# Scores ahead of values, masks and exponentials ahead of the split of the output, in every unit of an attention group

## What is computed

```python
q = (x @ w_q) ...            # 32 heads of 128; k, v: 8 heads, shared by 4 query heads
lk = (x @ w_lq @ w_lk) ...   # 32 latent keys; lv = (x @ w_lv), 32 latent values
q, k, lk = rope(q), rope(k), rope(lk)
attn = causal_softmax(q, k, v)       # s = q k^T * scale, masked, softmax, times v
lat = causal_softmax(q, lk, lv)
x = layernorm(x + attn @ w_o + lat @ w_lo)
```

## Time and profile before

| | |
|---|---|
| median of the runs | 2509.61 us |
| the profiled execution | 2513.95 us, of which the span of instructions is 2512.0 us |
| PE busy | 2453.2 us, 98% of the span |
| PE weight loads | 2067.0 us, 82% |
| DVE busy | 1717.3 us, 68% |
| ACT busy | 1132.0 us, 45% |
| POOL busy | 923.3 us, 37% |
| granted TensorE clock, mean | 0.995 of full speed |
| DMA | 226.24 MB, mean 90 GB/s |

### The profile page before, as it was taken

How to read it: one execution, slowest core, us unless ns; L and a number is a source line. 1 busy time by engine, 2 the same in 40 slices (tenths; PEclk the granted TensorE clock), 3 DMA queues, 4 the chain that set the end, 5 groups by cost and what they waited for, 6 DMA issues and landing times.

```text
span 2512.0 us, 40346 instructions
## 1 busy us (share of the span) xinstructions
PE 2453.2 (98%) x12264; PEld 2067.0 (82%) x12264; DVE 1717.3 (68%) x3589; ACT 1132.0 (45%) x2576; POOL 923.3 (37%) x696
## 2 busy tenths in 40 slices
PE   7799999999999999999999999999999999999998
PEld 6688888888888888888767888888888888888877
DVE  5676667767676767666577676766767677667656
ACT  3443535344444435444365453544445353544550
POOL 4334242433334242433443425243342425334210
PEclk9999999999999999999999999999999999999999
DMA  5223231322323232323424323222232323234411
GB/s 172 93 80 97 60 106 53 98 64 70 94 76 96 61 101 61 87 68 99 129 86 133 105 70 110 69 86 77 84 104 71 106 73 106 61 93 144 155 34 67
DMA packets 124406, 226.24 MB, mean 90 GB/s; under 512 B 13088, under 2 KB 21408, under 8 KB 124192
## 3 DMA queue, kind: packets, MB, share of 16 engines
q1 hardware_dynamic: 119552, 216.91, 28.8%
q10 hardware_dynamic: 4768, 8.39, 1.0%
HBM read 206.37 MB, written 18.87 MB: 90 GB/s over the span
## 4 chain that ended last, share of the span: by engine, by line
PE 93%; DVE 2%; issue 1%; ACT 1%; DMA 1%; POOL 1%; SPq 0%; PEldq 0%; DVEq 0%; ACTq 0%; POOLq 0%
PE bank_a L1217 16%; PE bank_a L1218 16%; PE bank_a L1219 16%; PE bank_b L1217 13%; PE bank_b L1219 13%; PE bank_b L1218 13%; PE bank_b L1270 5%; DMA w_raw<-wstream 1%; PE bank_b L1539 1%; POOL w_lo L426 1%; DVE probs L821 0%; POOL acc L445 0%; PE bank_b L1406 0%; ACT w_hi L490 0%; PE bank_b L1522 0%
## 5 line engine op out<-in xcount | busy, mean ns | idle before, releaser
L426 POOL TENSOR_TENSOR w_lo<-w_raw,w_hi 128x512 fp32r<-128x512 f32 x632 | 845.0, 1346 | 1400.1 <-ACT w_hi L490 1380.4
L490 ACT ACTIVATE w_hi<-w_raw 128x512 fp32r<-128x512 f32 x632 | 392.7, 626 | 298.0 <-DMA w_raw<-wstream 115.3
L1217 PE MATMUL bank_a<-w_hi,o_hi 128*128 128x512 f32 x1024 | 410.2, 401 | 4.1 <-DVE o_lo L843 2.0
L1218 PE MATMUL bank_a<-w_lo,o_hi 128*128 128x512 f32 x1024 | 401.8, 392 | 0.0
L1219 PE MATMUL bank_a<-w_hi,o_lo 128*128 128x512 f32 x1024 | 401.6, 392 | 0.0
L527 ACT ACTIVATE probs<-probs,row_min 128x512 f32<-128x512 f32 (+3 forms) x512 | 281.6, 552 | 245.6 <-DVE row_min L821 243.1
L838 DVE TENSOR_TENSOR pT_lo<-bank_b,pT_hi 128x512 fp32r<-128x512 f32 (+1 forms) x384 | 207.2, 595 | 238.0 <-ACT pT_hi L533 238.0
L537 ACT ACTIVATE o_hi<-bank_b 128x512 fp32r<-128x512 f32 x128 | 76.8, 600 | 452.0 <-PE bank_b L1219 452.0
L832 DVE TENSOR_SCALAR probs<-probs,row_inv 128x512 f32<-128x512 f32 (+3 forms) x512 | 260.9, 569 | 4.5
L1217 PE MATMUL bank_a<-xT_hi,w_hi 128*128 128x512 f32 x544 | 215.7, 396 | 18.0 <-POOL w_lo L426 15.2
L1219 PEld LDWEIGHTS bank_a<-w_hi,o_lo 128*128 128x128 f32 x1024 | 192.6, 188 | 41.5
(11 more groups left out here) (168 smaller groups left out, 4686.5 us busy)
## 6 DMA issues: line engine op xcount, KB each, us to landing
w_raw<-wstream SPq DMA_DIRECT2D x632, 256.0 KB, 2.7
stage<-ctx SPq DMA_DIRECT2D x32, 256.0 KB, 2.8
stage_w<-wf SPq DMA_DIRECT2D x32, 256.0 KB, 2.8
q_scratch<-stage_q SPq DMA_DIRECT2D x32, 128.0 KB, 1.7
wf_hi_scratch<-piece_hi SPq DMA_DIRECT2D x16, 256.0 KB, 3.0
wf_lo_scratch<-stage_w SPq DMA_DIRECT2D x16, 256.0 KB, 3.4
wf_hi<-wf_hi_scratch SPq DMA_DIRECT2D x8, 512.0 KB, 7.6
wf_lo<-wf_lo_scratch SPq DMA_DIRECT2D x8, 512.0 KB, 8.1
```

Source lines behind the costliest of these rows:

```text
L426: nc.gpsimd.tensor_tensor(w_lo[:, s], w_raw[:, r], w_hi[:, s].bitcast(F32), ALU.subtract).then_inc(lo_done, 1)
L490: nc.scalar.activation(w_hi[:, s], w_raw[:, r], ACT.Copy).then_inc(hi_done, 1)
L1217: nc.tensor.matmul(dst, still[0], move[0], start=start, stop=False)
L1218: nc.tensor.matmul(dst, still[0], move[1], start=False, stop=False)
```

## The change

Three pairs of calls change places, each in every unit. On PE the scores of unit u + 2 go ahead of the values of unit u, with the transposes and both parts where they were. On DVE the masks of unit u + 2 go ahead of the low part of the output of unit u. On ACT the exponentials of unit u + 2 go ahead of the high part of the output of unit u. Unit 6 has values and no scores to make, unit 7 neither, and both stay as they were. No instruction is added or removed, and no wait is written differently.

```diff
--- before.py
+++ after.py
@@ -677,8 +677,8 @@
                         if c % 2 == 0:
                             pT_high(G, u)
                         else:
+                            exponentials(G, u + 2) if u + 2 < UNITS else None
                             o_high(G, u)
-                            exponentials(G, u + 2) if u + 2 < UNITS else None
                         if b and not tg:
                             crossed(c)
                     if b and c in (12, 29):
@@ -989,10 +989,10 @@
                         add_part(b, p + u // 2, u // 2, chunk(b, g, C_PREV + 4 + 2 * u), False)
                     if u in (4, 6):
                         add_part(b, p + u // 2, u // 2 - 2, chunk(b, g, C_PREV + 4 + 2 * u), first)
+                    if u + 2 < UNITS:
+                        mask_scores(G, u + 2)
                     if u + 1 < UNITS:
                         o_low(G, u)
-                    if u + 2 < UNITS:
-                        mask_scores(G, u + 2)
                     if u < 2 and first and b:
                         for t in range(TT):
                             half_stats_of_r(t, u)
@@ -1464,9 +1464,10 @@
                     transposes(G, u)
                     if u < UNITS - 1:
                         part(2 * u + 3)
-                        values(G, u)
                     if u + 2 < UNITS:
                         scores(G, u + 2)
+                    if u < UNITS - 1:
+                        values(G, u)
 
             def last_output(b, i):
```

## The result

The changed kernel took 2500.36 us (median of five runs, 2496.32 to 2501.99). Five runs of the kernel before beside it gave 2510.13 (2509.36 to 2513.61). The ratio is 0.9955, with an interval of 0.9941 to 0.997: 7.5 to 14.8 us faster, around 11.3. Forecast were 7.5 us and 2502.1, with 2500.4 as the low end of the range. (The forecast counted from 2509.61, the median of three of these five runs.)

The account below looks back on a forecast made before the run. PE, busy 98% of the span, was taken as the bound, with gain from its waits in the two first groups. 5.4 + 0.9 + 1.2 = 7.5 us off the median 2509.61 gave 2502.1, range 2500.4 to 2506.5.

Parts of the forecast that it names:

- 5.4 for batch 0: Batch 0's first group: S(6) starts 5.4 us before the time V(4) had, a lead carried to the end.
- Batch 1's term of 0.9: Batch 1's first group: 0.9 us gained by S(6), which was V(4); bounds -0.6 and 2.2.
- S(4) starts 0.6 later than V(2) did: Batch 1's first group: o_low waits for ACT's exponentials, so pT_low(2) ends at 1324.1, not 1323.5, and S(4) starts 0.6 later.
- The mask wait is hidden, and o_low takes its place in part: First groups: V(u) covers the masks' 1.78 us; new waits of 0.3 to 1.8 us on o_low before O(1), O(2), O(3).
- 1.55 more: O(0) in batch 0's first group: 2.87 us at full clock instead of 4.41, besides starting 1.55 earlier.
- the clock falls all the same: Rival, chance 0.25: O(0) in batch 0 still runs at half speed; the gain there is 3.9 instead of 5.4, total 2503.6.
- I take the clock as kept: Batch 0's first group: one gap of 1.7 remains, dense matmuls until 107.5, so O(0) runs at full clock.
- The 14 other groups, 1.2: Ordinary groups: V(1)'s weights get pT_low(1) net 0.09 us sooner, 14 times, so 1.2 us; bounds 0 and 1.8.
- about 0.2 instead of 0.29: Sign: in other groups S(3)'s weights wait about 0.2 us for pT_low(1), where V(1)'s had waited 0.29.
- group period unchanged to 0.1: Sign that the forecast is right: the period of the groups stays unchanged to 0.1 us.
- the 0.05 behind the values: PE: the block after V pays 0.05; now the part instead of S, so nothing; if both paid, 112 units, 5.6 worse.
- Slower: Rival, chance 0.08: in the 14 groups o_high delays pT_high(1), V(1)'s place moves 0.52 later in each; 2515.4 at worst.

Follow-up runs that it names:

- after: The profiled execution of the changed kernel, with all three exchanges in every unit: 2501.99 us.
- after_again: The changed kernel run once more, unedited, on another chip: 2499.53 us, ratio 0.9954 to the kernel before.
- rest_only: The kernel before with the three exchanges in the 14 ordinary groups alone, the old order in the two first groups: 2507.17 us, ratio 0.9986.
- before_pool_late: The kernel before, with POOL's low part of chunk 32 in batch 1's first group held until DVE has clipped the weight piece: 2508.0 us (one run).
- pe_dve: The kernel before with the exchanges on PE and DVE, ACT keeping o_high ahead of the exponentials: 2507.28 us (one run).
- dve_act_only: The kernel before with the exchanges on DVE and ACT, PE keeping values ahead of scores: 2521.79 us (one run).
- before: The profiled execution of the kernel before, with the old order everywhere: 2513.95 us.
- before_warm: The kernel before with 8 extra matmuls into an unused bank ahead of T(0) in both first groups: 2509.32 us, ratio 0.9995.

## Why the prediction came out as it did

**Which step failed.** The waits went and came as forecast; two terms of the sum were too small. The range's low end was added up from 5.4 for batch 0, 2.2 for batch 1 and 1.8 for the 14 other groups, the last two at their bounds. The stretches of the 14 groups gave 2.95, beyond their bound: the prediction counted one place per ordinary group, and neither the same place in unit 5 of the first groups nor any other step. Batch 1's term of 0.9, with its step "S(4) starts 0.6 later than V(2) did", measured 1.96: S(4) came 0.45 sooner. The 0.04 us by which the median lies below the range are themselves far inside the noise.

**The mask wait is hidden, and o_low takes its place in part: right.** In batch 0 T(1) to T(4) lost their waits of 1.06 to 1.42 (the first two in the earlier trace rows), and O(1) to O(3) wait 0.61, 0.30 and 0.61 in batch 0 and 0.62, 0.34 and 1.19 in batch 1, inside the forecast 0.3 to 1.8. The steps to O(1) in after, first DVE, then ACT:
```profile
113.86 0.69 DVE L821 CUSTOM_DVE_ANT_0 probs<-bank_b,mask_sb 128x512 f32<-128x512 f32 x1 [1.10 <-PE bank_b L1219]
...
117.39 0.69 DVE L843 TENSOR_TENSOR o_lo<-bank_b,o_hi 128x512 fp32r<-128x512 f32 x1 [1.80 <-ACT o_hi L537]
...
120.92 1.28 DVE L832 TENSOR_SCALAR probs<-probs,row_inv 128x512 f32<-128x512 f32 x4
122.11 0.69 DVE L821 CUSTOM_DVE_ANT_0 probs<-bank_b,mask_sb 128x512 f32<-128x512 f32 x1
```
```profile
114.59 0.72 ACT L527 ACTIVATE probs<-probs,row_min 128x512 f32<-128x512 f32 x1 [4.28 <-DVE row_min L821]
...
116.79 0.57 ACT L537 ACTIVATE o_hi<-bank_b 128x512 fp32r<-128x512 f32 x1
```
From first mask to o_high 2.93 (forecast 2.92), from o_high to O(1) 1.35 (forecast 1.37), mask behind the start of S(3) 1.03 (forecast 0.95).

**Batch 0, 5.4: 4.9 in this pair, 5.7 where the clock did as assumed, about 4.0 for the order alone.** The prediction took the clock as low until about 105.5, 3.5 us behind the start of S(2). In after it stayed at its lower level until about 106.4, 5.6 behind; S(2) and V(0) needed 6.6 us and not 5.5, and O(0) came 9.21 behind the start of S(2) and not 8.32. In after_again it rose at about 105.3, 3.8 behind, and the steps came out as written. PE of after_again, O(0), S(3) and S(6); S(2) starts at 101.52:
```profile
109.86 0.47 PE L1217 MATMUL bank_a<-w_hi,o_hi 128*128 128x512 f32 x1 [1.05 <-issue]
...
112.70 0.39 PE L1217 MATMUL bank_b<-keys_hi,q_hi 128*128 128x512 f32 x1
...
137.32 0.39 PE L1217 MATMUL bank_b<-keys_hi,q_hi 128*128 128x512 f32 x1
```
That is 8.34, 11.18 and 35.80 behind S(2), forecast 8.32, 11.17 and 36.17, and 5.74 shorter than before from V(0) or S(2) to V(4) or S(6). From S(3) to S(6) it took 24.6 in both executions and not 25.0: in the turn of unit 2 normalise took 1.28 (the DVE rows above) and not 1.94. There too POOL stood beside it before (its low part from 124.95 to 126.24, normalise from 125.38) and hardly after (until 121.00, normalise from 120.92).
What isn't shown is that "1.55 more", for the clock in O(0), belongs to the change. The matmuls did keep the full clock, 0.39 apiece, in after and in every other kernel with all three exchanges there, and the rival "the clock falls all the same" fell. But "I take the clock as kept" was set against a kernel before that always loses it, and rest_only and before_pool_late have its order and kept it too. rest_only and after have their half clock in the same windows before O(0) (low until about 106.8 and 106.4, 18.5 and 18.4 behind S(0)), and differ by 59.94 - 55.99 = 3.95 from S(0) to T(5): in this one pair, that is the order alone. pe_dve, with 3.23 us of waiting before O(0), lost it, and so did dve_act_only with 2.19.

**Batch 1, 0.9: 1.96.** The failed step is "S(4) starts 0.6 later than V(2) did". From S(2) to S(4) it took 22.37, where V(0) to V(2) had taken 22.82: 0.45 sooner, 1.05 better than forecast. The order's loss on DVE was real but smaller: the statistics began 17.47 behind the start of S(2) against 17.22, 0.25 later and not 0.6. And the clipping, taken at its 1.17 of before, was 0.70 shorter without POOL beside it, which before_pool_late confirms. The part behind it, from V(2) or S(4) to V(4) or S(6), gave 18.76 to 17.25, 1.5, as "win that back and 0.9 more" had it.

**The 14 other groups, 1.2: 2.95, over the bound of 1.8.** The wait itself was right: "about 0.2 instead of 0.29". PEld of after, the later group of the earlier trace rows, now the weights of S(3):
```profile
391.55 0.19 PEld L1217 LDWEIGHTS bank_b<-keys_hi,q_hi 128*128 128x128 f32 x1 [0.20 <-DVE pT_lo L838]
```
Waits of PEld, 170 to 1150 us, before and then after:
```profile
PEld bank_b L1217 <- DVE pT_lo L838: 2.0, 7, 0.3
PEld bank_b L1270 <- DVE row_min L821: 1.6, 7, 0.2
```
```profile
PEld bank_b L1217 <- DVE pT_lo L838: 1.4, 7, 0.2
```
Windows of the seven groups, after and then before:
```profile
144.16:1151.25 1007.09, 1007.09 (x5097) 860.41 (x5096) 707.49 (x1488) 451.13 (x1073) 371.62 (x283) 1.00 0.26 79
```
```profile
150.45:1158.94 1008.49, 1008.49 (x5097) 860.17 (x5097) 701.89 (x1487) 457.05 (x1078) 371.37 (x282) 1.00 0.27 79
```
By the spacing of the transposes, a mean over seven groups, T(1) to T(2), the step with the pT_low wait, went from 10.27 to 10.14 in batch 0 and from 10.26 to 10.14 in batch 1: 1.8 us in 14 groups, where I had 1.2 and a bound of 14 x 0.13. (No row of the prediction gives that 0.13, but it is what came.) The same wait before V(5) of both first groups went too, 10.27 to 10.07 from T(5) to T(6), 0.20 each; the prediction has no term for it. The other 0.8 us are steps that lost 0.01 to 0.03 apiece. The view of PEld shows one more kind of wait that went, 0.23 us on the row minima ahead of T(1)'s weights, which the waits of PE don't show; but T(0) to T(1) lost only 0.01, so it doesn't explain the 0.8, whose cause is open. The period went from 142.60 to 142.43, and the sign "group period unchanged to 0.1" wasn't met.

Who pays the 0.05 behind the values came out as the prediction had it: in after the first matmul of S(3) lasts 0.39, and the first of the parts behind V(4) and V(5) 0.45 and 0.44. Its price for the other case, with 112 units, counts all eight units of a group; only six have scores beside values, so it would be 84 x 0.05 = 4.2 us.

**The rest stays open.** Taken at equal clock, the order gives 3.95 in batch 0's first group, 1.96 + 0.12 in batch 1's and 2.95 in the others: 9.0 us, 1.5 above the forecast: 1.75 more in the ordinary groups, 1.2 more in batch 1, 1.45 less in batch 0. With O(0)'s clock counted it is 10.5. The comparisons give 11.3 (7.5 to 14.8) and 11.6 (8.3 to 15.1). What lies between 9.0 and these can be noise, or that the new order loses the clock less often. O(0) kept it in five of five profiled executions with all three exchanges there and no extra matmuls, and in two of three of the kernels with the old order there; that is too few to tell.

**Slower: fell.** No PE wait on pT_low came in ordinary groups. dve_act_only lost 0.6 us a group in batch 1, but at V(2), behind DVE's clipping, and not at V(1) behind o_high. POOL and SP, which nothing was moved past, showed no new wait on the path.

## What to carry to other kernels

Where one engine is the wall, put the block whose successor runs on other engines (scores, then masks) ahead of the block that needs nothing more (values), and then move the other engines' queues in the same way: the exchange on PE alone cost 83 us, on the others alone 12 us (one run each), together it gained 11. An effect in a steady loop is bounded badly by the waits of one view: here they gave 0.09 us of a period that fell by 0.17, and in 14 groups that was worth more than a wait in a group that runs once. Ask the weight loads too, and compare the loop's steps one by one. Where a number comes from an instruction with a neighbour on a shared port, ask what stands beside it in the new order.

## What the runs showed of the hardware that I had not expected

- A VectorE `TENSOR_SCALAR` on 128x512 float32 in SBUF took 0.47 us alone and 1.17 with a GpSimd `TENSOR_TENSOR` started 0.40 ahead of it; begun 0.04 behind, it took 1.52. It ended 0.28 to 0.30 behind POOL's end each time. The four pieces of normalise took 1.28 with 0.08 of it beside POOL and 1.94 with 0.86 of it beside POOL.
- The places at which TensorE's clock falls to half differ between executions of the same order of work: O(0) ran at 0.63 us a matmul in before and at 0.40 in rest_only, a matter of 1.5 us; the context product's place is worth 2.45. Single executions of the changed kernel ran from 2496.3 to 2502.0, of the kernel before from 2504.8 to 2514.1. Differences under 2 us were not told apart by medians of five.
- With extra matmuls in the wait before T(0), batch 1's context product ran at full clock in three of three executions (4.50 us from first to last in before_warm, against 7.17 before), without them in six of eleven; that is too few to call it their doing, and the medians show no gain.
